# Second network of a four-network graph kernel: degree factors by broadcast DMA, destination side one quarter ahead, a piped reading pass, and a fused first sweep

## What is computed

```python
norm = deg_inv_sqrt[src] * deg_inv_sqrt[dst]
h = relu(segment_sum((x @ W1)[src] * norm, dst) + b1)      # 32 -> 128 features
h = relu(segment_sum((h @ W2)[src] * norm, dst) + b2)      # 128 -> 128
h = relu(segment_sum((h @ W3)[src] * norm, dst) + b3)      # 128 -> 32
```

## Time and profile before

| | |
|---|---|
| three runs, median (lowest, highest) | 8515.5 us (8512.02 to 8523.6) |
| the profiled execution, its own time | 8527.12 us |
| its span | 8525.3 us |
| PE, DVE, ACT, POOL busy over the span | 67%, 55%, 29%, 39% |
| granted TensorE clock, mean | 0.824 of full speed |
| stages P3, T3, P4 together | 951 us |

### The profile page before, as it was taken

One profiled execution on the slowest core, in us unless ns is written; L12 is line 12 of the kernel. 1 busy time (PEld: TensorE's weight loads), 2 busy tenths in 40 slices (PEclk: granted clock), 3 DMA queues, 4 the chain that ended last, 5 costly groups with the idle time before them and its releaser, 6 DMA issues.

```text
span 8525.3 us, 71449 instructions
## 1 busy us (share of the span) xinstructions
PE 5690.7 (67%) x21484; PEld 2626.3 (31%) x21492; DVE 4696.7 (55%) x6891; ACT 2495.5 (29%) x4074; POOL 3350.0 (39%) x3658
## 2 busy tenths in 40 slices
PE   2997894431488745576766667675675799999950
PEld 1434442221243311222222222223354444444420
DVE  5563332232444466686867778684375556666640
ACT  1663331110132211111111111112321266666630
POOL 3777745565433333343434353445406200000026
PEclk9997886655799867787878888787797899999975
DMA  2004557896543478797978788796203100000000
GB/s 77 11 9 142 196 207 88 74 78 53 92 91 64 83 237 249 207 264 209 258 214 255 233 231 263 207 266 82 33 1 26 15 10 15 13 15 15 9 18 19
DMA packets 535938, 986.79 MB, mean 116 GB/s; under 512 B 99055, under 2 KB 288259, under 8 KB 535172
## 3 DMA queue, kind: packets, MB, share of 16 engines
q1 hardware_dynamic: 424900, 911.36, 29.8%
q0 software_dynamic: 110656, 70.87, 18.3%
HBM read 778.66 MB, written 203.60 MB: 115 GB/s over the span
## 4 chain that ended last, share of the span: by engine, by line
PE 37%; DMA 18%; POOL 15%; issue 13%; DVE 11%; ACT 5%; SPq 1%; POOLq 0%; DVEq 0%; ACTq 0%
POOL gathered L787 9%; DMA gathered<-table,idx_slot 6%; DMA blocks<-net 5%; PE ps L917 5%; PE ps L1305 4%; DMA ring<-net 4%; PE ps L979 4%; POOL pair_slot L787 2%; PE ps L1067 2%; DVE ring L2093 2%; PE ps L1068 2%; POOL last_of L802 2%; POOL out_dram L901 1%; PE ps L1072 1%; PE ps L1412 1%
## 5 line engine op out<-in xcount | busy, mean ns | idle before, releaser
L787 POOL DMA_INDIRECT gathered<-table,idx_slot x2156 | 2099.4, 974 | 1583.0 <-DVE ring L2093 880.7
L2093 DVE TENSOR_TENSOR ring<-ring,ps 128x1024 f32<-128x1024 f32 (+2 forms) x1008 | 1073.0, 1083 | 499.3 <-DMA ring<-net 464.6
L979 PE MATMUL ps<-ring,mats 128*32 128x512 f32 (+2 forms) x4032 | 709.5, 657 | 372.6 <-DVE ring L2093 311.9
L917 PE MATMUL ps<-mats,gathered 128*128 128x128 f32 x1029 | 217.3, 343 | 1051.1 <-DMA gathered<-table,idx_slot 1001.2
L896 POOL COPY idx_slot<-idx_run_end 128x16 int32<-128x16 int32 (+2 forms) x14 | 2.7, 195 | 1556.3 <-SPq L769 1538.5
L917 PE MATMUL ps<-mats,w 128*128 128x128 f32 x1323 | 279.1, 354 | 449.8 <-DVE w L2556 249.9
L917 PEld LDWEIGHTS ps<-mats,gathered 128*128 128x128 f32 x1029 | 146.5, 171 | 1221.0 <-DMA gathered<-table,idx_slot 1087.9
L780 POOL COPY idx_slot<-idx_row 128x16 int32<-128x16 int32 (+2 forms) x154 | 33.6, 218 | 1085.4 <-SPq L548 1040.5
L2160 DVE SCALAR_TENSOR_TENSOR x_block<-ps,bias,blocks 128x512 f32<-128x512 f32 x300 | 224.7, 749 | 384.3 <-PE ps L1072 384.1
L979 PEld LDWEIGHTS ps<-ring,mats 128*32 128x32 f32 x4032 | 156.0, 125 | 873.4 <-issue 542.4
L2093 DVE TENSOR_TENSOR blocks<-blocks,ps 128x1024 f32<-128x1024 f32 (+2 forms) x336 | 357.4, 1085 | 62.8 <-DMA blocks<-net 58.2
(11 more groups left out here) (279 smaller groups left out, 12241.8 us busy)
## 6 DMA issues: line engine op xcount, KB each, us to landing
ring<-net SPq DMA_DIRECT2D x792, 512.0 KB
blocks<-net SPq DMA_DIRECT2D x264, 512.0 KB
net<-ring SPq DMA_DIRECT2D x176, 512.0 KB, 2.8
table<-w SPq DMA_DIRECT2D x165, 256.0 KB, 2.9
gathered<-table,idx_slot POOLq DMA_INDIRECT x2352, 3.4
ring<-net SPq DMA_DIRECT2D x144, 256.0 KB
x_sp<-x_block SPq DMA_DIRECT2D x79, 256.0 KB, 8.4
x_block<-x_sp SPq DMA_DIRECT2D x79, 256.0 KB, 5.4
```

The costliest lines, as they stand in the source:

```text
L787: pool.indirect_dma_start(dests(k), None, rows, bass.IndirectOffsetOnAxis(ap=dst[:, k:k + 1], axis=0)).then_inc(done, 16)
L917: last = nc.tensor.transpose(dst[:, k * P:k * P + P], src[:, k * P:k * P + P], mat["ident"])
L979: last = mm(message[t * D:t * D + D, 0:wd(i)], adders[2 * m + c], ring[slot][:, c * wd(i):(c + 1) * wd(i)], start=(m == 0 and c == 0), sto ...
L2093: v.tensor_tensor(pair, pair, state, ALU.mult).then_inc(sig["pr"][S_], 1)
```

## The change

1. T3 and P4 no longer spread degrees by a matmul. SP loads each quarter's row of degree factors with a DMA that reads one DRAM row and writes it to all 128 partitions (`to_broadcast`), into `deg_wide` (four pairs of tiles in `ring` and `blocks4`). In T3 these DMAs take the place of POOL's L869. The DVE products then read two SBUF tensors where one operand was in PSUM.
2. Sweep t = 0 of T3 is fused into P3, one block behind it. Sweeps 1 to 3 follow as before.
3. P4 runs over steps (block, quarter), with `w2` one step behind and `w3` two steps behind on PE; the next block's first steps start while the last block's last layers are open. DVE finishes a block (`third_out`) after its part of step t = 2 of the next block.
4. The destination side works on quarter (t + 1) mod 4 where the source side works on t. `w1` is multiplied with the 32 rows of its quarter alone, and `w3` writes the 32 output rows of its quarter alone.

```diff
-                    mm(fit(pB[par], i), mat[f"spread{t}"], fit(db[par], i), start=True, stop=True
-                       ).then_inc(sig["bd"][par], 1)
...
+            def wide_degrees_in(t, i):
+                par, n = i % 2, q.n("bm", i % 2, i // 2, t * halves(EB)[i % 2])
+                sp.wait_ge(sig["bm"][par], n + CREDIT)
+                settle(sp)
+                sp.dma_start(fit(deg_wide[par][S_], i), d_sp[S_, t * D:t * D + 1, col(i)].to_broadcast([P, wd(i)])
+                             ).then_inc(dma["ld_d4"][par], 16)
+
+            def wide_rows_out(t, i):
+                par = i % 2
+                sp.wait_ge(sig["b4"][par], q.n("b4", par, i // 2, t * halves(EB)[par]) + 1 + CREDIT)
+                settle(sp)
...
+            for n, (t, i) in enumerate(sweeps):
+                if n + 1 < len(sweeps):
+                    wide_degrees_in(*sweeps[n + 1])
+                wide_rows_out(t, i)
```

The fused stage on PE and DVE, and the steps of P4:

```diff
+            for i in range(EB):
+                light_head(i)
+                if i:
+                    products(0, i - 1)
+                if i > 1:
+                    wide_rows(0, i - 2)
...
+            def third_layer(i, t):
+                for u in SPACES:
+                    pe.wait_ge(sig["q6"][u], q.n("q6", u, i, t) + 1 + CREDIT)
+                    if t == 0:
+                        pe.wait_ge(sig["g"][u], q.n("g", u, i) + CREDIT)
+                for u in SPACES:
+                    cols = quarter_rows(side_quarter(u, t))
+                    mm(fit(pD[u], i)[cols, :], wts[:, WEIGHTS.index(f"w3_{side_quarter(u, t)}"), cols], fit(conv_second[t % 2][u], i),
+                       start=True, stop=True).then_inc(sig["q7"][u], 1)
+
+            steps = [(i, t) for i in range(EB) for t in range(T)]
+            for n, (i, t) in enumerate(steps):
+                wide_in(i, t)
+                first_layer(i, t)
+                if n > 0:
+                    second_layer(*steps[n - 1])
+                if n > 1:
+                    third_layer(*steps[n - 2])
...
+            for i in range(EB):
                 for t in range(T):
-                    for u in SPACES:
...
+                    join(i, t)
+                    if t == 2 and i:
+                        third_out(i - 1)
+            third_out(EB - 1)
```

More of the change, by code:

```diff
@@ L217, in plan @@
     n4 = tuple(T * h for h in halves(EB))
-    add("T3", "ld_d4 b1 b1r bd bk bm b3 b3t b4 st_tab4", blocks=n4)
-    add("P4", "ld_d g q_head q1 q1r qd q2 q3 q4 q5 q6 q7", s="scan", times=Q4, alternate="ld_gd", wide=True)
+    add("T3", "ld_d4 b1 b1r bk bm b3 b3t b4 st_tab4", blocks=n4)
+    add("P4", "ld_d ld_x ld_d1 g q_head q1 q1r q2 q3 q4 q5 q6 q7", s="scan", times=dict(Q4, ld_d=2, ld_x=2), alternate="ld_gd", wide=True)
     add_tab("T4")
@@ L722, in _ @@
             pass_over(sp, "P2")
[L723 to L733, removed]
+            q, q3 = p_["T3"], p_["P3"]
@@ L734, in _ @@
+            sweeps = [(t, i) for t in range(1, T) for i in range(EB)]
+            wide_degrees_in(*sweeps[0])
+            wide_rows_out(0, EB - 1)
+            for n, (t, i) in enumerate(sweeps):
+                if n + 1 < len(sweeps):
+                    wide_degrees_in(*sweeps[n + 1])
+                wide_rows_out(t, i)
             for par in (0, 1):
@@ L864, in _ @@
             pass_over(pool, "P3")
[L865 to L870, removed]
             q4 = p_["P4"]
@@ L1388, in _ @@
+            for t in range(1, T):
+                products(t, 0)
+                for i in range(EB):
+                    if i + 1 < EB:
+                        products(t, i + 1)
+                    wide_rows(t, i)
             for par in (0, 1):
@@ L1436, in _, with wide_in, first_layer @@
-            sweep(pe, EB, body)
+            side_quarter = lambda u, t: (t + u) % T
+            def wide_in(i, t):
+                pe.wait_ge(dma["ld_g4"][t % 2], 16 * (2 * col_of(i) // P + (t // 2 + 1) * q_of(i)))
+                landed(pe, "ld_gd", t % 2, q.n("ld_gd", t % 2, i, t // 2))
+                for u in SPACES:
+                    pe.wait_ge(sig["q3"][u], q.n("q3", u, i, t) + CREDIT)
+                    turn(fit(pA[u], i), G[t % 2][u], q_of(i)).then_inc(sig["q_head"][u], 1)
+            def first_layer(i, t):
+                for u in SPACES:
+                    pe.wait_ge(sig["q1r"][u], q.n("q1r", u, i, t) + CREDIT)
+                for u in SPACES:
+                    rows = quarter_rows(side_quarter(u, t))
+                    mm(fit(pB[u], i), wts[rows, WEIGHTS.index(f"w1_{side_quarter(u, t)}"), :], h[u][rows, col(i)],
+                       start=True, stop=True).then_inc(sig["q1"][u], 1)
@@ L1437, in _ @@
+            steps = [(i, t) for i in range(EB) for t in range(T)]
+            for n, (i, t) in enumerate(steps):
+                wide_in(i, t)
[4 more added lines that the diff above has]
+                    third_layer(*steps[n - 2])
+            second_layer(*steps[-1])
+            third_layer(*steps[-2])
+            third_layer(*steps[-1])
             tables("T4", "P4")
@@ new lines, in third_out @@
+            def third_out(i):
+                for u in SPACES:
+                    dve.wait_ge(sig["q7"][u], q.n("q7", u, i, T - 1) + 1 + CREDIT)
+                    landed(dve, "ld_d1", u, q.n("ld_d1", u, i))
+                    v.tensor_tensor(blk(h[u], i), fit(pD[u], i), fit(d_turn[i % 3][u], i), ALU.mult).then_inc(sig["g"][u], 1)
+                dve.wait_ge(sig["g"][S_], q.n("g", S_, i) + 1 + CREDIT)
+                run_sums(q, i, blk(h[S_], i))
+            for i in range(EB):
+                for t in range(T):
+                    join(i, t)
+                    if t == 2 and i:
+                        third_out(i - 1)
```

238 lines of the change are left out of this document (126 added, 112 removed).

## The result

The changed kernel takes 8389.7 us (median of 4 runs, 8379.17 to 8397.92) against 8519.55 us for the kernel before on the same chip (4 runs): a ratio of 0.9843, 95% interval 0.9824 to 0.9861. It is 130 us faster; forecast were 8316 us and 200 us. Its profiled execution took 8391.05 us, with a span of 8389.1 us.

What follows compares the result with a forecast made beforehand. It took P3 as bound by gathers, T3 and P4 by PE. Gains of 29 us (T3: 41.4 - 12.6) and 171 us (P4) sum to 200, from 8527.1 to 8327, less 11.6: 8316 us; own range 8290 to 8340, wider 8270 to 8400.

Steps and rivals of the forecast that it cites:

- Fused sweep: T3's sweep 0 run behind P3's blocks: its first sweep 1 product moves from 2278.7 to 2237.3 us, gaining 41.4 us.
- the 200 idle us: In P3, bound by gathers: idle time on PE, ACT and DVE, some 200 us, in which added work was to hide.
- My own sign for being wrong: Prediction wrong if P3 grows over 5 us, T3's blocks come each 3.0 us or less, or P4's steps await gathered rows.
- 3.55 us per block: T3, sweeps 1 to 3: loop of load behind store, product, scan, transpose, copy, 7.1 us for two blocks; sweeps 12.6 us longer.
- no longer binds: T3, sweeps 1 to 3: PE loses L1375's spread, 0.9 us per block, and so stops setting the block time.
- the one through PE and ACT: T3, sweeps 1 to 3: loop of scan, transpose, copy, `w1`, relu, product, 5.4 us over two blocks, 2.7 per block.
- 5.25 us per step: P4, both sides of one quarter: set by a loop in which DVE's sum frees `pA` for the next step's transposes.
- the hole: P4, once per block: `w3` waits for `third_out(i - 1)`, delaying step 3's transposes; 9.4 us, making a block 25.2 us.
- P4's ends: P4's two small blocks, paced by gathers, take 30.6 us (bounds 26 and 40); last block and drain take 21.5 us.
- POOL paces P4: Rival, chance 0.27: P4 gathers blocked through DVE's two-SBUF work; a block takes 29.7 us, 41 us more, 8357.
- DMA or PE's clock binds P4: Rival, chance 0.08: loads land late or granted clock falls with PE's share; blocks of 33 to 36 us, 8393 to 8426.
- T3's load hides: Rival, chance 0.10: T3's degree load lands fast enough to hide, below 1.5 us; 28 us less, 8288.

## Why the prediction was right and wrong

- **The sign and the range** were right: 8389.7 lies in 8270 to 8400, though beyond my forecast's own 8290 to 8340.
- **Fused sweep, 41.4 us.** About right: 39 us by undoing it. Wrong in it is "So it costs nothing while the 200 idle us cover it": I had looked at POOL's instructions, which were not slowed (185 us busy in P3, as before), and not at the DMA engines' time for what they issue. P3 grew by 8.2 us against before and by 6 against the unfused version. My own sign for being wrong, P3 longer by over 5 us, is met.
- **Sweeps 1 to 3, "3.55 us per block".** The ring was found and exists, but measured 4.2: from 2323.33 the product (0.69), scan (1.28), transposes, copy, store at 2327.30, load at 2328.10, and 3.8 to 3.9 us until the data of such a load is used, not 3.05; the transposes took 1.06, not 0.60, at 1.2 GHz. The 3.05 was taken from a load of 128 different rows, and for that it was right: with such loads in place of the broadcast the median is 3.0. The Trainium skill (DMA: Bandwidth & Descriptors, Anatomy of one DMA) has a fit for a DMA issued by GpSimd; used for this load from SP it gives 2.6 us by estimate, and the row has 3.6, further off than my value.
- **The step that failed outright** is that PE, without L1375, "no longer binds". It took PE's durations as given. Removing the spread and cutting `w1` to 32 rows left PE at 1.2 GHz for all of T3, and `w1` went from 1.13 to 2.07 us: PE with ACT's copy became a second ring of 4.15. The three sweeps are 37.5 us longer than before (161.6 us from first product to last, against 124.1), where I had 12.6. That the clock could fall was in the prediction only for P4, as a rival with 0.08, and only "as PE's share does". Here the records have PE 81% busy, more than the 79% of a T3 sweep before, at half the clock. Part of that 81% is the low clock itself, at which `w1` lasts 2.07 us instead of 1.13; but with 128 rows, the same 265 matmul records in as long a time had a mean clock of 0.75. The Trainium skill (TensorE: Matmul & The Clock Gate, Part 1) calls the low clock the default that activity releases. Busy time in the records does not measure that activity here.
- **Which of the two made T3 miss.** Either alone would have been nearly enough: with the clock at 0.75 and the load late the stretch is 171.4 us, with the load early and the clock at 0.50 it is 161.5, with both mended 119.0. The ring through the load was priced at 3.55 us per block and the one through PE and ACT at 2.7; both measured 4.15, and each hid the other.
- **P4, "5.25 us per step".** 5.0, and PE sets it, not the ring I counted: its records leave no gap.
- **P4, "9.4 us" for the hole.** Place and cause right, 12.2 measured, since PE is at 1.2 GHz for the step behind it: transposes, `w1` and `w2` take 3.2 us more, less small change. That, not slowed gathers, makes the block 27.2 us: three steps of 5.0 and one of 12.2. Eleven blocks: 13 us more than forecast.
- **P4's ends.** From the first gather (2413.30) to the first full block's transposes (2453.80) pass 40.5 us, not 30.6, with PE at 0.50, where the start of P4 before had 0.84. The wait of 8.3 us for the first rows is no part of it: before it was 7.3. The eleven blocks, to the last one's transposes at 2762.65, took 309 us, not 286: 13 by the hole, 6.8 by one stall of POOL that I had not (its cause is open; the kernel before has one of 8.5 us in P4), and 3 in the first ones. The end took 22.3, near the 21.5. These make the 34 us that P4 misses.
- **The rivals.** The time fell between *POOL paces P4* and *DMA or PE's clock binds P4*, and belongs to neither as written: gathers were slowed by 3% at most, and cutting the DMA load alone gained 5.5 us, within the spread. The clock's part of the second rival came true, in T3 above all, where I did not have it. *T3's load hides* was shown by its own experiment not to be enough: with the load hidden, T3 gains 11 to 17 us, not 28; the 28 and more come only with the clock.
- **DMA, 86% busy, "so it should not bind, but it is near".** Right: 0.83, and cutting it gains 6 us at most; once the hole is gone it costs, since the same cut then gives 26 us (367.5 to 341.6, on two chips).

What stays open: how far the clock alone, without the late rows, sets P4's block; and whether P4's own 32-row products hold its clock down, as the one in T3 does: no version has them on 128 rows.

## What to carry to other kernels

When work is taken off an engine, price what is left at the clock that the engine will then have: look at the granted clock of the stage for which the work was removed, and of a stage where the engine is as thinly loaded. When removing a wait gains nothing, look for a second ring of the same length before giving the idea up: in T3 two edits worth 7 and 17 us alone were worth 56 together. And before buffers are added to run further ahead, read the DMA engines' share: near 0.9, here, it bought only longer landings.

## What the runs showed of the hardware

- A stage with PE 81% busy by its records stood at 1.2 GHz for 160.6 us; with `w1` on 128 rows instead of 32, all else equal, the mean granted clock was 0.75 and PE's busy time fell from 129.8 to 98.7 us.
- With the DMA engines at 1.00 for 20 us, they moved 145 GB/s, less than the 204 GB/s of the 20 us before at 0.92; two issues of 256 KB on SP then lasted 4.8 us instead of 0.9.
- A load of 256 KB that reads one DRAM row for 128 partitions had its data used 3.8 us after its issue on SP, one that reads 128 rows 3.0 us (medians of 33 blocks of T3). In P4, at a DMA share of 0.83 and 0.82, the stage was as long with either, within its spread.
- Different chips took 8520 and 9131 to 9143 us for the same kernel, with most of the difference in the first quarter of the program, and these three stages within 3.5% of each other.
